# Mixture-of-experts stage: transposing an expert's inner values inside the next expert's gate and up product

## The reference, cut to what matters

```
for e in 0..63:                       # x_e: the 128 gathered rows of expert e, 128 x 512
    gate = x_e @ w_gate[e]            # 512 x 192
    up   = x_e @ w_up[e]              # 512 x 192
    h    = silu(gate) * up            # 128 x 192
    y    = h @ w_down[e]              # 192 x 512
    out[rows of e] += weight_e * y
```

## Time and profile before

| | us |
|---|---|
| median of 3 runs | 2829.46 |
| lowest and highest run | 2822.42, 2834.62 |
| profiled execution, its own time | 2822.21 |
| its span, first to last instruction | 2820.4 |
| TensorE's first transpose of the expert stage | 2443.59 |
| end of TensorE's last product of the stage | 2785.65 |

### The profile page before, as it was taken

One profiled execution on the slowest core, in us unless ns is written; L12 is line 12 of the kernel. 1 busy time (PEld: TensorE's weight loads), 2 busy tenths in 40 slices (PEclk: granted clock), 3 DMA queues, 4 the chain that ended last, 5 costly groups with the idle time before them and its releaser, 6 DMA issues. The chain is left out here.

```text
span 2820.4 us, 48637 instructions
## 1 busy us (share of the span) xinstructions
PE 2595.4 (92%) x17264; PEld 2094.0 (74%) x17291; DVE 1695.9 (60%) x3810; ACT 1291.2 (46%) x3417; POOL 857.2 (30%) x852
## 2 busy tenths in 40 slices
PE   7999987799999899999799999999999996399994
PEld 5666754689998688888688888888888886155552
DVE  6767688744344666666676666666667665622221
ACT  4777776222222444444555555555555553022221
POOL 3344322000000555555222222222222221155452
PEclk9999999899999899999899999999999998699997
DMA  3110022300011555556721522331142127599996
GB/s 136 49 46 24 21 69 63 108 28 19 23 46 60 187 184 183 195 187 195 236 60 57 157 64 72 104 107 46 53 143 55 45 88 251 167 294 296 296 296 111
DMA packets 227280, 340.07 MB, mean 121 GB/s; under 512 B 24801, under 2 KB 111201, under 8 KB 226529
## 3 DMA queue, kind: packets, MB, share of 16 engines
q1 hardware_dynamic: 209728, 293.56, 32.9%
q0 software_dynamic: 14912, 39.85, 6.5%
q10 hardware_dynamic: 2400, 3.55, 0.4%
HBM read 230.56 MB, written 110.53 MB: 121 GB/s over the span
## 5 line engine op out<-in xcount | busy, mean ns | idle before, releaser
L2069 POOL TENSOR_SCALAR a_prob<-a_prob,a_rinv 128x640 f32<-128x640 f32 (+3 forms) x256 | 253.5, 990 | 742.7 <-DVE a_rinv L2231 742.7
L2221 DVE TENSOR_REDUCE a_mx<-a_s_ps 128x1 f32<-128x640 f32 (+3 forms) x256 | 262.2, 1024 | 249.0 <-PE a_s_ps L2141 242.9
L2093 ACT ACTIVATE a_probT<-a_t_ps 128x512 fp32r<-128x512 f32 (+3 forms) x512 | 237.2, 515 | 350.4 <-PE a_t_ps L2149 350.4
L2237 DVE TENSOR_TENSOR a_probT<-a_t_ps,a_probT 128x512 fp32r<-128x512 f32 (+3 forms) x512 | 276.6, 582 | 45.2 <-ACT a_probT L2093 44.4
L2084 ACT ACTIVATE a_prob<-a_s_ps,a_nb,a_rs 128x640 f32<-128x640 f32 (+3 forms) x256 | 268.0, 1047 | 9.7 <-DVE a_nb L2222 9.7
L137 PE MATMUL a_o_ps<-a_probT,a_v 128*128 128x256 f32 x832 | 244.4, 294 | 0.0
L138 PE MATMUL a_o_ps<-a_probT,a_v 128*128 128x256 f32 x832 | 232.7, 280 | 0.0
L139 PE MATMUL a_o_ps<-a_probT,a_v 128*128 128x256 f32 x832 | 232.3, 279 | 0.0
L2149 PE MATMUL a_t_ps<-kept_ident,a_prob 128*128 128x128 f32 x1664 | 225.7, 274 | 2.1 <-POOL a_prob L2069 2.1
L2149 PEld LDWEIGHTS a_t_ps<-kept_ident,a_prob 128*128 128x128 f32 x1664 | 194.7, 141 | 25.0 <-POOL a_prob L2069 2.7
L736 PEld LDWEIGHTS a_bank<-kept_ident,a_prob 128*128 128x128 f32 x1024 | 112.4, 143 | 120.0 <-ACT a_prob L580 97.9
(11 more groups left out here) (307 smaller groups left out, 7087.9 us busy)
## 6 DMA issues: line engine op xcount, KB each, us to landing
expert_ring<-in_w_gate SPq DMA_DIRECT2D x64, 384.0 KB, 18.6
expert_ring<-in_w_up SPq DMA_DIRECT2D x64, 384.0 KB, 20.2
expert_ring<-in_w_down SPq DMA_DIRECT2D x64, 384.0 KB, 23.4
l_q_hi<-p_turned SPq DMA_DIRECT2D x64, 256.0 KB, 2.4
l_q_lo<-p_turned SPq DMA_DIRECT2D x64, 256.0 KB, 2.1
h_split<-l_q_hi SPq DMA_DIRECT2D x62, 256.0 KB, 3.2
h_split<-l_q_lo SPq DMA_DIRECT2D x62, 256.0 KB, 3.8
l_v_hi<-p_vs SPq DMA_DIRECT2D x32, 256.0 KB, 2.2
```

The source lines that it names most:

```text
L2069: pool.tensor_scalar(prob[:, k % 4, 0:w], prob[:, k % 4, 0:w], rinv[:, k % 4:k % 4 + 1], 1.0, ALU.mult, ALU.mult).then_inc(s["weighted"], 1)
L2093: act.activation(probT[0][:, pair % 2, i * 4:i * 4 + n, k % 2], t_ps[i][:, 0:n * P].rearrange("p (m n) -> p m n", n=P), ACT.Copy).then_inc ...
L2221: step(dve.tensor_reduce(mx[:, k % 4:k % 4 + 1], s_ps[:, k % 2, 0:w], AX.X, ALU.max))
L2237: dve.tensor_tensor(probT[1][:, pair % 2, i * 4:i * 4 + n, k % 2], t_ps[i][:, 0:n * P].rearrange("p (m n) -> p m n", n=P), probT[0][:, pai ...
```

## The change

`turn_h(e-1)` is issued between the second and the third of the four matmuls of `gate_up(e)`, instead of behind the fourth. In round 64, which has no `gate_up`, it stays where it was. Nothing else is moved: the same instructions run, with the same waits and the same operands.

```diff
                     if e >= 2:
                         pe.wait_ge(s["h_made"], e - 1)
                     for k in range(KC):
+                        if k == 2 and e:
+                            turn_h(e - 1)
                         mm = pe.matmul(gu_ps[e % 2][:, 0:2 * F1], xT[:, e % 2, k], wgu[:, u, :, k], start=(k == 0), stop=(k == KC - 1))
                     mm.then_inc(s["gu_done"], 1)
...
                 for e in range(E + 1):
                     if e < E:
                         gate_up(e)
-                    if e:
+                    else:
                         turn_h(e - 1)
                     turn_x(e + 1)
                     if e:
```

## The result

The changed kernel took 2810.62 us in the median of 9 runs (2807.71 to 2816.49), the kernel before 2829.46 (2822.42 to 2834.62). The ratio is 0.994, 95% interval 0.9929 to 0.9952. So it is faster by 0.6%, 14 to 20 us; 2813.0 was predicted. The profiled execution took 2810.49, with a span of 2808.7.

What follows compares the result with a forecast made beforehand. TensorE's list was taken to set the pace, with the transfers near behind. A gain of 16.9 us less a 0.4 stall gave 16.5, taking the median from 2829.5 to 2813.0 us; range 2806 to 2824.

Steps and rivals of the forecast that it cites:

- The hole is the wait for `hT`, 0.26 us per round: Between the last transpose of x and y on TensorE: starts 0.38 apart instead of 0.12, so 0.26 us gained per round.
- Cost inside the product 0.22, no lag behind a transpose: Between passes 4 and 5: the moved transposes lengthen the product by 0.22 us, and pass 5 starts 0.11 behind the last.
- Rival 3: From the second transpose of h to pass 5: weight loads wait behind transposes, 0.27 us more per round, 2846; chance 0.05.
- Slack of `h` 0.9, of `hT` over 1: At the moved transposes `h` is ready 0.9 us early; at y's weight load `hT` has over 1 us to spare.
- Sum of TensorE 16.9: Over the stage's rounds: 0.26 us in each of rounds 1 to 62, 16.1, plus round 63's gain, sum 16.9 us.
- Stall at the last expert 0.4: At the last product: weights wanted at 2761.0 land at 2761.4, so TensorE stalls 0.4 us, once.
- The landing was to slip by 6.8 us: The last weight load: gathers and scatters pulled forward delay its landing by 6.8 us, from 2754.6 to 2761.4.
- The share given to scatters: In the transfers' time per expert: 1.23 us for a scatter, of 2.2 us for gather and scatter together.
- Rival 1: At the last expert: heavier scatters make the weights late, a stall of 5.5 us, time 2818; chance 0.15.
- Rival 2: On GpSimd: scatters waiting for the one two rounds before set the round; from landings of 10.5 on, 2829; chance 0.06.
- Rival 4: In the whole kernel: the change does nothing, the same hole remains, time within 5 us of 2829; chance 0.04.

Runs made afterwards that it cites:

- twice_before: The kernel before, with ScalarE's copy of `hT` done twice, first into a spare tile; its round measured 5.53 us.
- twice_after: The changed kernel, with ScalarE's copy of `hT` done twice, first into a spare tile; its stage measured 325.9 us.
- down_late: The kernel before, with down(e-2) instead of down(e-1) behind the transposes of h; rounds of 5.00 us, the whole 10 us slower than the changed kernel.
- k1: The changed kernel, with the two transposes of h behind the first of the four matmuls instead of the second; its stage measured 325.4 us.
- k3: The changed kernel, with the two transposes of h behind the third matmul instead of the second; its stage measured 325.4 us.
- late4_after: The changed kernel, with each weight load from expert 17 on waiting for four more rounds of TensorE; it cost 8.9 us of stage.
- no_scatter: The changed kernel, with the scatters of experts 8 to 61 left out; round and stage did not move, loads came every 5.57 us.

## Why the prediction was right, point by point

- *The hole is the wait for `hT`, 0.26 us per round.* Right. Rounds went from 5.254 to 4.99. twice_before makes the hole larger by the 0.27 that is added, twice_after does not, and down_late closes it with the product left whole.
- *Cost inside the product 0.22, no lag behind a transpose.* Right: weights load at the start of the transpose before (2602.56) and the pass follows after 0.11. Rival 3 (0.38) is refuted. The Trainium skill, "TensorE: Matmul & The Clock Gate", Part 3, What overlaps and what doesn't, has a weight load overlap only matmuls in other row groups. Here it overlaps one in the same rows, as the rows of the round at 2602.56 show, so the measurement decides against it.
- *Slack of `h` 0.9, of `hT` over 1.* Right. `h` ends at 2600.88 + 0.35 = 2601.23 and its load comes at 2602.13; `hT` has 1.06. k1 and k3 use up most of these and lose nothing.
- *Sum of TensorE 16.9.* Measured 16.3. The difference lies at the start of the stage, where the granted clock was 0.50 (1.2 GHz): the first two products begin 6.25 us apart before (2445.41, 2451.66) and 6.83 after (2449.42, 2456.25). From 2450 to 2455 the clock was already 1.00 before the change, but still 0.50 after it. The change does not alter this round up to there, so these 0.6 us are the clock's and not the change's.
- *Stall at the last expert 0.4.* The term that was mis-sized, though it is small in the sum: no profile of the changed order with its usual loads shows a stall. The landing was to slip by 6.8 us. Measured from the stage's start, the last load lands at 311.0 before and at 305.5, 309.6, 315.2 and 313.2 in the changed kernel, k1, k3 and twice_after: a slip between -5.5 and +4.2. The share given to scatters was about three times too large, and it is scatters of which the faster TensorE adds three; of gathers it adds 1.5. A slip of (3.04 x 0.4 + 1.5 x 1.8) / (1 - 0.4 / 4.99) = 4.3 would follow from the measured split. Want and landing were 22.5 us apart, and the want moved by 333.5 - 317.9 = 15.6, so 22.5 - 15.6 - 4.3 = 2.6 us would be left, about what k3 and twice_after have. The rest differs from profile to profile by +-5 us, as much as the effect, and nothing here shows why. That this profile has 12.5 us left is in part luck.
- *Rival 1, weights late by several us.* It did not occur. late4_after shows its mechanism, with loads made late.
- *Rival 2, the scatter chain.* I gave it 0.06 and read its headroom as 1.1 us. That reading was wrong: the next scatter begins 0.8 us behind the landing, so 9.98 - 0.8 - 8.9 = 0.3 us was left at the median landing. As a cost in the changed kernel the chain did not occur. As a mechanism it is there: landings beyond 9.2 us now hold GpSimd up, by up to 4.1 us, and six gathers ahead absorb it. In the changed kernel the largest lag is that of the last gather but one (expert 62), and in k3 that of the last (4.7), so these profiles do not show whether the lag would stay bounded in a longer stage.
- *The kernel as a whole.* 2813.0 forecast, 2810.6 measured. Rival 4 (nothing changes) is excluded by the round of 4.99.

## What to carry to other kernels

Read holes in a busy engine from the distance between starts, not from its busy share or from the waits view: here TensorE was busy for 50 of 50 us, the view gave 12.5 us to the wait, and 16 could be had. A step whose result another engine must turn around before it is used belongs far enough ahead that this turnaround is hidden; any place in the window between its input and its use is equally good, and outside it costs at once. Then count what a faster engine consumes: the change took 16 us out of the stage and, with it, 10 to 20 of the 22.5 us of margin of the weight loads, by profile, and all the headroom of the scatters. A second change of this size would meet these first. And a margin read from one profile is one sample: here it differs by 10 us between kernels of the same round.

## What the runs showed of the hardware

- TensorE loads weights for an fp32 matmul while an fp32 transpose in the same rows is in flight, and the switch from transposes to a product costs no more than the next transpose would: 0.11 us from load to start (2602.56, 2602.67). The other way, the transposes of h start 0.32 us behind the last pass (2602.13, 2602.45), the distance between two passes of the product.
- With gathers, scatters and loads together the transfers of the changed kernel moved 293 to 305 GB/s in stretches of 50 us at a share of 1.06. By the estimate from no_scatter, a gather of 0.295 MB took about 1.8 us per expert from the loads and a scatter of 0.262 MB 0.3 to 0.4; by bytes they would be nearly alike.
- GpSimd issued a scatter 0.80 us behind the landing that it waited for, and TensorE loaded weights less than 0.1 us behind theirs (late4_after, expert 61: 2770.7, 2770.78).
- A weight load behind a wait for VectorE came 0.06 us after it in one order of the list and 0.23 in another. Why is open.
